# Attention of a small vision tower on one core: keys copied in six pieces by image, keys turned behind the probabilities, output product ahead of the scores

## The chip, the cores and the metric

One core of a Trainium2 chip runs the whole kernel. The metric is the device time of one execution in microseconds (us). Within a core the engines run their own instruction queues in order and meet at semaphores: PE is TensorE (matrix products and transposes), PEld its weight loads, DVE is VectorE, ACT is ScalarE, POOL is GpSimd, SP is SyncE, which issues most DMAs.

## The reference, cut to what matters

```python
h = tokens(x)                      # 32 images x 38 rows of 256: two class rows, 36 patches
h = h + attn(layernorm(h))         # 16 heads of 16
h = h + ffn(layernorm(h))          # 8 experts, two for each row, rotation, gate

def attn(x):                       # N = 32, L = 38, H = 16, D = 16
    q, k, v = x @ Wq.T, x @ Wk.T, x @ Wv.T      # each split into heads
    q, k = layernorm(q, gq, bq), layernorm(k, gk, bk)   # over the 16 of a head
    scores = where(causal, q @ k.T, -1e30)
    return softmax(scores) @ v @ Wo.T + bo
```

All of it is in fp32. The change touches `attn` alone, and there only who copies the keys and in which order the work of several tiles is issued.

## The kernel before, in words

The rows are worked in NT = 11 tiles of three images (114 rows; the last has two images). Embedding, the projections of all tiles and most of the head norms come first. Then attention runs as a software pipeline over tiles, and after it come the second norm, the experts in 26 slots, the rotation and the output.

In attention each engine runs its own `attn_step(t)` for t = 0 to 10: tiles 0 and 1 written out, 2 to 7 in a loop of two tiles a turn, 8 to 10 written out. For a tile:

- POOL multiplies the queries with their reciprocal deviations into three copies, one for each image (`norm`, L283 on POOL), spreads the values (`spread`, L431) and adds up the three images of the result (`gather_images`, L442, L443). DVE does the same to the keys (`norm_k`, L283 on DVE).
- PE transposes queries (`turn_q`, L1379) into PSUM banks 0 and 1, keys (`turn_k`, L1393) into banks 2 and 3: eight blocks of 96 rows, image i in partitions 32i to 32i+31.
- ACT copies the queries to `qd_sb` in three pieces, one for each image, 32 partitions by 304 (`keep_q`, L563). The keys go to `kc_sb`; there each image has two copies, a = 0 and a = 1, whose scales and biases blank the other head of a pair. ACT copies bank 2 (the first four blocks) in six pieces of 32x152 (`keep_k`, L572), three for a = 0 ahead of the probability copies and three for a = 1 behind them; DVE copies bank 3 in six pieces (`keep_k`, L893). `ka_kept` and `kv_kept` count the tiles that ACT and DVE have kept.
- PE makes the scores in two halves (`scores`, L1403 the mask, L1406 the products), in banks 4 and 5; DVE takes the row maximum and subtracts it (`shift`, L925, L927); ACT takes the exponential of each half (`exp_half`, L580).
- PE transposes the probabilities (`turn_probs`, L1417) into banks 0 and 1, ACT copies them in two parts (`keep_pT`, L586, L588), PE multiplies with the values (`values`, L1430), DVE divides by the sums and picks each row's image (`select`, L940, L943, L948).
- PE transposes the result (`turn_att`, L1313, on `att_sb`) into bank 2, ACT copies it (`keep_attT`, L594), PE multiplies with Wo into bank 3 (`output`, L1448), and DVE adds the residual and takes statistics (`finish`, L931, L779).

Banks 2 and 3 are thus shared: keys of tile t+2, then the turned result of tile t-1, and the output of tile t-2. The waits keep them apart: `turn_att(t)` waits for `ka_kept` of tile t+3, `output(t)` for `kv_kept` of tile t+4, `turn_k` for the copies of the turned result and for the residual add of earlier tiles.

What sets the order is the written order of the steps on each engine. Before the change it is, on PE: turn_q(t+2), turn_k(t+2), scores(t+1), turn_probs(t), output(t-2), values(t), turn_att(t-1). On ACT: keep_q(t+2), keys a = 0 of t+2, keep_pT(t), keys a = 1, exp halves of t+1, keep_attT(t-1), and in steps 8 and 9 a scaling of the generators (L615). On DVE: keep_k(t+2), shift(t+1), finish(t-2), norm_k(t+3), select(t).

Of the kernel before, what the change touches and what calls it, by code (L numbers as in the profile page):

```python
# [13 lines left out]
B, SEQ, D = 32, 38, 256  # L14
IPT = 3
# [44 lines left out]
def vit_kernel(nc, patches, w_tok, w_qkv, w_o, w_pre, w1, w2, b2, gens, gens_t,  # L60
# [6 lines left out]
    with ctx:  # L67
# [137 lines left out]
        q_kept, ka_kept, kv_kept, v_spread = sem("q_kept"), sem("ka_kept"), sem("kv_kept"), sem("v_spread")  # L205
# [76 lines left out]
        def scaled(eng, dst, src, r):  # L282
            return eng.tensor_tensor(wide(dst), thrice(src), r.unsqueeze(2).broadcast_to([T, NH * IPT, HD]), ALU.mult)  # L283

# [231 lines left out]
        def _(act):  # L516
# [50 lines left out]
            def keep_k(t, s, a):  # L567
                act.wait_ge(k_turned, t + 1)
                for i in range(IPT):
                    r, c = slice(32 * i, 32 * i + 32), slice(SEQ * i, SEQ * (i + 1))  # L570
                    kc = kc_sb[r, s * CH:s * CH + CH // 2].rearrange("p (n a m) -> p n a m", a=2, m=SEQ)
                    last = nc.scalar.activation(kc[:, :, a, :], bank[2][r, :].rearrange("p (n m) -> p n m", m=128)[:, :, c], ACT.Identity,  # L572
                                                scale=col_sb[r, C_GK + a:C_GK + a + 1], bias=col_sb[r, C_BK + a:C_BK + a + 1])
                if a == 1:
                    last.then_inc(ka_kept, 1)
# [20 lines left out]
            def attn_step(t, s):  # L596
                if ahead(t, 2):
                    keep_q(t + 2, s)
                    keep_k(t + 2, s, 0)
                keep_pT(t)  # L600
                if ahead(t, 2):
                    keep_k(t + 2, s, 1)
                if ahead(t, 1):
                    exp_half(t + 1, 1 - s, 0)
                    exp_half(t + 1, 1 - s, 1)
                if behind(t, 1):
                    keep_attT(t - 1)
# [10 lines left out]
            for t in range(EARLY, NT):  # L618
# [3 lines left out]
                if t == 9:  # L622
                    keep_k(0, 0, 0)
            keep_k(0, 0, 1)
# [5 lines left out]
            keep_k(1, 1, 0)  # L630
            keep_k(1, 1, 1)
# [124 lines left out]
        def _(dve):  # L756
# [127 lines left out]

            def keep_k(t, s):
# [3 lines left out]
                for i in range(IPT):  # L889
                    r, c = slice(32 * i, 32 * i + 32), slice(SEQ * i, SEQ * (i + 1))  # L890
                    kc = kc_sb[r, s * CH + CH // 2:(s + 1) * CH].rearrange("p (n a m) -> p n a m", a=2, m=SEQ)
                    for a in range(2):
# [875 lines left out]
```

## Time and profile before

| what | value |
|---|---|
| median of 3 runs | 359.38 us (359.34 to 362.27) |
| the profiled execution | 359.24 us, span 356.7 us, mean granted clock 0.966 |
| PE busy | 320.9 us, 90% |
| DVE busy | 219.9 us, 62% |
| ACT busy | 184.6 us, 52% |
| POOL busy | 140.8 us, 39% |

The profile cuts the span into 40 equal slices of 8.9 us; a digit is the busy share of a slice in tenths:

```profile
PE   5999999729999999987989599999999999998794
DVE  0275467997789999987888478776322212113674
ACT  0212455846688989855423785243434556550451
POOL 2001815041445665373004248757752644522000
PEclk9999999955799999999999999999999999999999
```

Attention lies in slices 8 to 17, about 70 to 160 us. The busy shares are averages over stages; starts of instructions, a tile apart, say more of one stage.

### The profile page before, as it was taken

To read this page: it belongs to the slowest core of one execution; us is meant where nothing else is said; L and a number is where in the kernel's file an instruction comes from. 1 tells how busy PE (TensorE), PEld (TensorE's weight loads), DVE (VectorE), ACT (ScalarE), POOL (GpSimd) and SP (SyncE) were. 2 spreads that over 40 slices of the span, in tenths; PEclk is the share of its full clock that TensorE was granted. 3 is DMA by queue.
4 is the path that set the end of the run, shared out by engine and by line. 5 is a ranking of instruction groups with operands and counts; after the bars stand their busy time and mean duration, and the time that the engine had idled before them with its cause. 6 is when DMAs were issued, how large, how long until landed. Compare 5 with 4: busy or idle time off the path is not lost.

```text
span 356.7 us, 6514 instructions
## 1 busy us (share of the span) xinstructions
PE 320.9 (90%) x1954; PEld 272.7 (76%) x1954; DVE 219.9 (62%) x590; ACT 184.6 (52%) x432; POOL 140.8 (39%) x147
## 2 busy tenths in 40 slices
PE   5999999729999999987989599999999999998794
PEld 4987556528888888875778498899988999986673
DVE  0275467997789999987888478776322212113674
ACT  0212455846688989855423785243434556550451
POOL 2001815041445665373004248757752644522000
PEclk9999999955799999999999999999999999999999
DMA  8571411123111110009622366535442567641443
GB/s 253 195 275 55 187 56 56 55 91 131 48 47 48 47 46 17 2 1 408 237 90 80 95 210 178 174 108 169 131 157 75 180 193 194 200 137 59 144 145 103
DMA packets 21120, 45.29 MB, mean 127 GB/s; under 512 B 2086, under 2 KB 14436, under 8 KB 20836
## 3 DMA queue, kind: packets, MB, share of 16 engines
q1 hardware_dynamic: 17444, 36.79, 31.3%
q0 software_dynamic: 2496, 6.82, 6.2%
q10 hardware_dynamic: 1152, 1.32, 1.2%
q8 instruction: 15, 0.25, 0.3%
q14 instruction: 13, 0.11, 0.1%
HBM read 37.71 MB, written 7.22 MB: 126 GB/s over the span
## 4 chain that ended last, share of the span: by engine, by line
PE 71%; issue 7%; DMA 6%; DVE 5%; SPq 3%; ACT 3%; POOL 3%; DVEq 0%; POOLq 0%; ACTq 0%
PE banks L1573 11%; PE banks L1582 10%; PE banks L1515 9%; PE banks L1289 7%; PE banks L1430 6%; PE banks L1406 5%; SPq L372 3%; PE banks L1334 3%; PE banks L1448 3%; PE banks L1379 3%; PE banks L1393 3%; DMA qk_sb<-y_rows 3%; PE banks L1486 2%; DMA qn_sb<-z_rows,gidx_sb 2%; PE banks L1417 2%
## 5 line engine op out<-in xcount | busy, mean ns | idle before, releaser
L1573 PE MATMUL banks<-qn_sb,w_sb 128*128 128x128 f32 x416 | 51.1, 276 | 1.2 <-ACT qn_sb L671 1.0
L1573 PEld LDWEIGHTS banks<-qn_sb,w_sb 128*128 128x128 f32 x416 | 48.6, 192 | 2.1 <-ACT qn_sb L671 1.2
L1582 PE MATMUL banks<-w_sb,sq_sb 128*128 x208 | 49.0, 379 | 0.0
L671 ACT ACTIVATE qn_sb<-banks,col_sb 128x128 f32<-128x128 f32 x52 | 21.0, 454 | 43.9 <-PE banks L1560 39.8
L1204 DVE TENSOR_TENSOR pT_sb<-banks,p_sb 128x256 f32<-128x256 f32 x26 | 11.0, 424 | 52.0 <-PE banks L1582 45.9
L484 POOL DMA_INDIRECT y_rows<-pT_sb,sidx_sb x26 | 25.7, 990 | 43.4 <-DVE pT_sb L1204 42.5
L1582 PEld LDWEIGHTS banks<-w_sb,sq_sb 128*128 128x128 f32 x208 | 38.1, 190 | 4.4
L682 ACT ACTIVATE sq_sb<-banks,col_sb 128x128 f32<-128x128 f32 x104 | 32.3, 364 | 16.4 <-PE banks L1573 13.7
L478 POOL DMA_INDIRECT qn_sb<-z_rows,gidx_sb x26 | 27.9, 1073 | 20.5 <-PE banks L1560 11.5
L572 ACT ACTIVATE kc_sb<-banks,col_sb 32x152 f32<-32x152 f32 x66 | 31.0, 470 | 1.1
L1289 PE MATMUL banks<-patch_sb,wtok_sb 128*128 128x252 f32 (+1 forms) x120 | 26.1, 380 | 4.3 <-DMA wtok_sb<-in_w_tok 4.3
L1289 PEld LDWEIGHTS banks<-patch_sb,wtok_sb 128*128 128x128 f32 x120 | 22.7, 207 | 6.6 <-DMA wtok_sb<-in_w_tok 4.3
L893 DVE TENSOR_SCALAR kc_sb<-banks,col_sb 32x152 f32<-32x152 f32 x66 | 25.5, 423 | 2.6 <-PE banks L1393 2.3
L563 ACT ACTIVATE qd_sb<-banks,col_sb 32x304 f32<-32x304 f32 x33 | 19.7, 597 | 10.9 <-PE banks L1379 10.6
L442 POOL TENSOR_TENSOR att_sb<-p_sb 114x256 f32<-114x256 f32 x11 | 8.1, 738 | 38.8 <-DVE p_sb L948 38.8
L1430 PEld LDWEIGHTS banks<-vd_sb,pT_sb 114*114 114x114 f32 x132 | 19.1, 188 | 5.3 <-issue 3.9
L283 POOL TENSOR_TENSOR qn_sb<-qk_sb,wtok_sb 114x768 f32<-114x768 f32 x11 | 17.1, 1562 | 14.4 <-DVE wtok_sb L868 7.4
L1430 PE MATMUL banks<-vd_sb,pT_sb 114*114 114x147 f32 x132 | 20.9, 302 | 1.8 <-ACT pT_sb L586 1.8
L1406 PE MATMUL banks<-kc_sb,qd_sb 96*114 96x76 f32 x176 | 22.2, 275 | 0.0
L1406 PEld LDWEIGHTS banks<-kc_sb,qd_sb 96*114 96x114 f32 x176 | 22.2, 197 | 0.0
L1334 PE MATMUL banks<-wqkv_sb,h_sb 128*114 128x512 f32 x44 | 20.7, 592 | 0.0
L1379 PE MATMUL banks<-con_sb,qn_sb 114*96 114x114 f32 x88 | 12.1, 288 | 6.6 <-POOL qn_sb L283 6.6
(234 smaller groups left out, 635.2 us busy)
## 6 DMA issues: line engine op xcount, KB each, us to landing
w_sb<-in_w SPq DMA_DIRECT2D x26, 512.0 KB
w_sb<-in_w SPq DMA_DIRECT2D x1, 4096.0 KB, 12.7
vrep_sb<-v_rows SPq DMA_DIRECT2D x33, 114.0 KB
qk_sb<-y_rows SPq DMA_DIRECT2D x10, 228.0 KB
patch_sb<-in_patches SPq DMA_DIRECT2D x3, 756.0 KB, 4.4
v_rows<-v_sb SPq DMA_DIRECT2D x11, 114.0 KB
z_rows<-h_sb SPq DMA_DIRECT2D x11, 114.0 KB
out_rows<-h_sb SPq DMA_DIRECT2D x10, 114.0 KB
```

Source lines behind the costliest of these rows:

```text
L478: pool.indirect_dma_start(out=xs_sb[:, s * D:(s + 1) * D], out_offset=None, in_=z_dram, in_offset=bass.IndirectOffsetOnAxis(ap=gidx_sb[:, ...
L484: pool.indirect_dma_start(out=y_dram, out_offset=bass.IndirectOffsetOnAxis(ap=sidx_sb[:, j:j + 1], axis=0), in_=ys_sb[:, s * D:(s + 1) * D ...
L572: last = nc.scalar.activation(kc[:, :, a, :], bank[2][r, :].rearrange("p (n m) -> p n m", m=128)[:, :, c], ACT.Identity, scale=col_sb[r, C ...
L682: last = nc.scalar.activation(hidT_sb[:, s * HID + c * 128:s * HID + (c + 1) * 128], bank[2 + 2 * s + c // 2][:, (c % 2) * 128:(c % 2 + 1) ...
L893: last = nc.vector.tensor_scalar(kc[:, :, a, :], bank[3][r, :].rearrange("p (n m) -> p n m", m=128)[:, :, c], col_sb[r, C_GK + a:C_GK + a ...
L1289: return nc.tensor.matmul(embed_out(g, c), wtok_sb[:, k * D + c * 128:k * D + (c + 1) * 128], patch_sb[:, at + k * w:at + (k + 1) * w], st ...
L1334: last = nc.tensor.matmul(bank[4 + s][0:T, :], hT(t, k), wqkv_sb[:, k * 3 * D:k * 3 * D + 2 * D], start=(k == 0), stop=(k == 1))
L1406: last = nc.tensor.matmul(bank[4 + hf][0:T, n * 2 * SEQ:(n + 1) * 2 * SEQ], qd_sb[0:96, q0:q0 + T], kc_sb[0:96, k0:k0 + 2 * SEQ], start=Fa ...
L1430: last = nc.tensor.matmul(bank[6 + n // 3][0:T, n % 3 * IPT * VW:(n % 3 * IPT + w) * VW], pT_sb[0:w * SEQ, n * T:(n + 1) * T], vd_sb[0:w * ...
L1515: last = nc.tensor.matmul(dst[:, m * D:(m + 1) * D], xT[:, k * D + m * 128:k * D + (m + 1) * 128], y[:, k * D:(k + 1) * D], start=(k == 0) ...
L1573: last = nc.tensor.matmul(bank[2 + 2 * s + c // 2][:, (c % 2) * 128:(c % 2 + 1) * 128], w1_sb[:, w0:w0 + 128], xsT_sb[:, (2 * s + k) * 128 ...
L1582: last = nc.tensor.matmul(bank[6 + s][:, 0:D], hidT_sb[:, s * HID + k * 128:s * HID + (k + 1) * 128], w2_sb[:, ds(e * 4 * D + k * D, D)], ...
```

## The change

The keys of a tile are copied by image instead of by bank. A piece is now 32x304, over both banks: ACT takes image 0 (a = 0 and 1) and image 2 with a = 0, DVE image 2 with a = 1 and then image 1 with a = 0 and 1. A new semaphore, `k2_kept`, holds ACT's piece of image 2 until DVE's piece of the same image is done. Both key semaphores are now asked for in scores, output and turn_att. The order of the steps becomes, on PE: turn_q(t+2), output(t-2), scores(t+1), turn_probs(t), turn_k(t+2), values(t), turn_att(t-1); on ACT: keep_q(t+2), exp half 0 of t+1, keep_pT(t), exp half 1, keep_k(t+2), keep_attT(t-1); on DVE: finish(t-2), shift(t+1), keep_k(t+2), norm_k(t+3), select(t).

```diff
--- before.py
+++ after.py
@@ -202,7 +202,7 @@
         qk_made, v_made, qk_squared_cr, v_kept_cr, ss_set_cr = (
             sem("qk_made"), sem("v_made"), sem("qk_squared_cr"), sem("v_kept_cr"), sem("ss_set_cr"))
         rs_set, qn_set, kn_set, q_turned, k_turned = sem("rs_set"), sem("qn_set"), sem("kn_set"), sem("q_turned"), sem("k_turned")
-        q_kept, ka_kept, kv_kept, v_spread = sem("q_kept"), sem("ka_kept"), sem("kv_kept"), sem("v_spread")
+        q_kept, ka_kept, kv_kept, k2_kept, v_spread = sem("q_kept"), sem("ka_kept"), sem("kv_kept"), sem("k2_kept"), sem("v_spread")
         scored, shifted_cr, max_set, probs_set = sem("scored"), sem("shifted_cr"), sem("max_set"), sem("probs_set")
         p_turned, pT_kept, pv_made, rc_set, rci_set, sel_set = (
             sem("p_turned"), sem("pT_kept"), sem("pv_made"), sem("rc_set"), sem("rci_set"), sem("sel_set"))
@@ -282,6 +282,11 @@
         def scaled(eng, dst, src, r):
             return eng.tensor_tensor(wide(dst), thrice(src), r.unsqueeze(2).broadcast_to([T, NH * IPT, HD]), ALU.mult)
 
+        def k_part(s, i, a):
+            r = slice(32 * i, 32 * i + 32)
+            dst = kc_sb[r, s * CH:(s + 1) * CH].rearrange("p (n a m) -> p n a m", a=2, m=SEQ)[:, :, a, :]
+            return banks[1][r, :].rearrange("p (n m) -> p n m", m=128)[:, :, SEQ * i:SEQ * (i + 1)], dst, r
+
         def ahead(t, n):
             return not isinstance(t, int) or t + n < NT
 
@@ -564,15 +569,17 @@
                                                 scale=col_sb[r, C_GQ:C_GQ + 1], bias=col_sb[r, C_BQ:C_BQ + 1])
                 last.then_inc(q_kept, 1)
 
-            def keep_k(t, s, a):
+            def keep_k_part(s, i, a):
+                src, dst, c = k_part(s, i, a)
+                return nc.scalar.activation(dst, src, ACT.Identity, scale=col_sb[c, C_GK + a:C_GK + a + 1],
+                                            bias=col_sb[c, C_BK + a:C_BK + a + 1])
+
+            def keep_k(t, s):
                 act.wait_ge(k_turned, t + 1)
-                for i in range(IPT):
-                    r, c = slice(32 * i, 32 * i + 32), slice(SEQ * i, SEQ * (i + 1))
-                    kc = kc_sb[r, s * CH:s * CH + CH // 2].rearrange("p (n a m) -> p n a m", a=2, m=SEQ)
-                    last = nc.scalar.activation(kc[:, :, a, :], bank[2][r, :].rearrange("p (n m) -> p n m", m=128)[:, :, c], ACT.Identity,
-                                                scale=col_sb[r, C_GK + a:C_GK + a + 1], bias=col_sb[r, C_BK + a:C_BK + a + 1])
-                if a == 1:
-                    last.then_inc(ka_kept, 1)
+                keep_k_part(s, 0, 0)
+                keep_k_part(s, 0, 1)
+                act.wait_ge(k2_kept, t + 1)
+                keep_k_part(s, 2, 0).then_inc(ka_kept, 1)
 
             def exp_half(t, s, hf):
                 act.wait_ge(shifted_cr, 2 * t + hf + 3)
@@ -596,13 +603,13 @@
             def attn_step(t, s):
                 if ahead(t, 2):
                     keep_q(t + 2, s)
-                    keep_k(t + 2, s, 0)
-                keep_pT(t)
-                if ahead(t, 2):
-                    keep_k(t + 2, s, 1)
                 if ahead(t, 1):
                     exp_half(t + 1, 1 - s, 0)
+                keep_pT(t)
+                if ahead(t, 1):
                     exp_half(t + 1, 1 - s, 1)
+                if ahead(t, 2):
+                    keep_k(t + 2, s)
                 if behind(t, 1):
                     keep_attT(t - 1)
                 if isinstance(t, int) and t in (8, 9):
@@ -620,15 +627,13 @@
                 if t == 8:
                     keep_q(0, 0)
                 if t == 9:
-                    keep_k(0, 0, 0)
-            keep_k(0, 0, 1)
+                    keep_k(0, 0)
             root(1)
             nc.scalar.activation(al_sb[:, 78:79], con_sb[:, K_ZERO:K_ZERO + 1], ACT.Exp)
             keep_q(1, 1)
             exp_half(0, 0, 0)
             exp_half(0, 0, 1)
-            keep_k(1, 1, 0)
-            keep_k(1, 1, 1)
+            keep_k(1, 1)
             attn_tiles(act, attn_step)
 
 
@@ -882,17 +887,18 @@
                 k, r = qk_sb[0:T, ds(t * 2 * D + D, D)], rs_sb[0:T, ds((2 * t + 1) * RW, RW)]
                 scaled(nc.vector, kn_sb[0:T, s * IPT * D:(s + 1) * IPT * D], k, r).then_inc(kn_set, 1)
 
+            def keep_k_part(s, i, a):
+                src, dst, c = k_part(s, i, a)
+                return nc.vector.tensor_scalar(dst, src, col_sb[c, C_GK + a:C_GK + a + 1], col_sb[c, C_BK + a:C_BK + a + 1],
+                                               ALU.mult, ALU.add)
+
             def keep_k(t, s):
                 dve.wait_ge(k_turned, t + 1)
                 if behind(t, 2):
                     dve.wait_ge(scored, 2 * t - 2)
-                for i in range(IPT):
-                    r, c = slice(32 * i, 32 * i + 32), slice(SEQ * i, SEQ * (i + 1))
-                    kc = kc_sb[r, s * CH + CH // 2:(s + 1) * CH].rearrange("p (n a m) -> p n a m", a=2, m=SEQ)
-                    for a in range(2):
-                        last = nc.vector.tensor_scalar(kc[:, :, a, :], bank[3][r, :].rearrange("p (n m) -> p n m", m=128)[:, :, c],
-                                                       col_sb[r, C_GK + a:C_GK + a + 1], col_sb[r, C_BK + a:C_BK + a + 1], ALU.mult, ALU.add)
-                last.then_inc(kv_kept, 1)
+                keep_k_part(s, 2, 1).then_inc(k2_kept, 1)
+                keep_k_part(s, 1, 0)
+                keep_k_part(s, 1, 1).then_inc(kv_kept, 1)
 
             for t in range(EARLY):
                 qkv_step(t, t % 2)
@@ -955,12 +961,12 @@
                 stats(h1_sb, t)
 
             def attn_step(t, s):
+                if behind(t, 2):
+                    finish(t - 2)
+                if ahead(t, 1):
+                    shift(t + 1, 1 - s)
                 if ahead(t, 2):
                     keep_k(t + 2, s)
-                if ahead(t, 1):
-                    shift(t + 1, 1 - s)
-                if behind(t, 2):
-                    finish(t - 2)
                 if ahead(t, 3):
                     norm_k(t + 3, 1 - s)
                 if isinstance(t, int) and t == NT - 1:
@@ -1386,8 +1392,8 @@
                     pe.wait_ge(kv_kept, t)
                 if behind(t, 4):
                     pe.wait_ge(attT_kept, t - 3)
-                if behind(t, 5):
-                    pe.wait_ge(h1_added_c1, t - 3)
+                if behind(t, 4):
+                    pe.wait_ge(h1_added_c1, t - 2)
                 for n in range(NH // 2):
                     at = s * IPT * D + n * 96
                     last = nc.tensor.transpose(banks[1][0:96, n * 128:n * 128 + T], kn_sb[0:T, at:at + 96], identT)
@@ -1397,8 +1403,9 @@
 
             def scores(t, s):
                 pe.wait_ge(q_kept, t + 1)
+                pe.wait_ge(ka_kept, t + 1)
+                pe.wait_ge(kv_kept, t + 1)
                 for hf in range(2):
-                    pe.wait_ge(ka_kept if hf == 0 else kv_kept, t + 1)
                     pe.wait_ge(shifted_cr, 2 * t + hf + 1)
                     nc.tensor.matmul(bank[4 + hf][0:T, 0:CH // 2], idb_sb[0:T, :], mask8, start=True, stop=False, skip_group_check=True)
                     for n in range(4):
@@ -1436,12 +1443,14 @@
                 pe.wait_ge(att_set, t + 1)
                 if more:
                     pe.wait_ge(ka_kept, t + 4)
+                    pe.wait_ge(kv_kept, t + 4)
                 turn_two(bank[2], att_sb[0:T, s * D:(s + 1) * D]).then_inc(att_turned, 1)
 
             def output(t, more=True):
                 pe.wait_ge(attT_kept, t + 1)
                 if more:
-                    pe.wait_ge(kv_kept, t + 5)
+                    pe.wait_ge(ka_kept, t + 4)
+                    pe.wait_ge(kv_kept, t + 4)
                 if behind(t, 1):
                     pe.wait_ge(h1_added_c1, t + 1)
                 for k in range(2):
@@ -1452,12 +1461,13 @@
             def attn_step(t, s):
                 if ahead(t, 2):
                     turn_q(t + 2, s)
-                    turn_k(t + 2, s)
+                if behind(t, 2):
+                    output(t - 2, ahead(t, 1))
                 if ahead(t, 1):
                     scores(t + 1, 1 - s)
                 turn_probs(t, s)
-                if behind(t, 2):
-                    output(t - 2, ahead(t, 2))
+                if ahead(t, 2):
+                    turn_k(t + 2, s)
                 values(t, s)
                 if behind(t, 1):
                     turn_att(t - 1, 1 - s, ahead(t, 2))
```

## Rows read from the trace of the kernel before

**Rows 1.** Stretches: start:end, length, busy us of each engine, clock, DMA share, GB/s.

```profile
127.95:135.37 7.42, 7.14 (x61) 6.45 (x61) 7.08 (x19) 6.58 (x14) 4.33 (x4) 1.00 0.14 46
```

**Rows 2.** Timeline of DVE, one tile: start us, us, line, operation.

```profile
128.96 1.02 DVE L948 TENSOR_TENSOR p_sb<-banks,rci_sb 114x432 f32<-114x432 f32 x2
...
129.90 2.35 DVE L893 TENSOR_SCALAR kc_sb<-banks,col_sb 32x152 f32<-32x152 f32 x6
...
132.28 0.47 DVE L925 TENSOR_REDUCE mx_sb<-banks 114x8 f32<-114x304 f32 x1
...
132.78 0.47 DVE L927 TENSOR_TENSOR p_sb<-banks,mx_sb 114x304 f32<-114x304 f32 x1
...
134.06 0.41 DVE L931 TENSOR_TENSOR h_sb<-banks,hb_sb 114x256 f32 x1
...
136.37 1.02 DVE L948 TENSOR_TENSOR p_sb<-banks,rci_sb 114x432 f32<-114x432 f32 x2
```

**Rows 3.** Timeline of PE, same tile; PE busy times overlap, ends are modelled.

```profile
127.54 0.41 PE L1313 MATMUL banks<-con_sb,att_sb 114*128 114x114 f32 x2
...
127.85 0.98 PE L1379 MATMUL banks<-con_sb,qn_sb 114*96 114x114 f32 x8
...
129.53 0.29 PE L1403 MATMUL banks<-maskb_sb,idb_sb 114*114 114x304 bf16 x1
...
131.32 0.75 PE L1417 MATMUL banks<-con_sb,p_sb 114*114 114x114 f32 x6
...
132.35 1.09 PE L1448 MATMUL banks<-wo_sb,attT_sb 128*114 128x256 f32 x4 [0.28 <-issue]
...
133.27 1.75 PE L1430 MATMUL banks<-vd_sb,pT_sb 114*114 114x147 f32 x12
...
134.95 0.41 PE L1313 MATMUL banks<-con_sb,att_sb 114*128 114x114 f32 x2
...
135.20 0.94 PE L1379 MATMUL banks<-con_sb,qn_sb 114*96 114x114 f32 x8
```

**Rows 4.** Timeline of ACT, same tile.

```profile
128.96 1.82 ACT L563 ACTIVATE qd_sb<-banks,col_sb 32x304 f32<-32x304 f32 x3 [0.61 <-PE banks L1379]
...
132.25 0.55 ACT L586 ACTIVATE pT_sb<-banks 114x456 f32<-114x456 f32 x1
...
133.08 1.44 ACT L572 ACTIVATE kc_sb<-banks,col_sb 32x152 f32<-32x152 f32 x3
...
134.54 0.80 ACT L580 ACTIVATE p_sb<-p_sb 114x304 f32<-114x304 f32 x2
...
135.48 0.36 ACT L594 ACTIVATE attT_sb<-banks 128x228 f32<-128x228 f32 x1
```

**Rows 5.** Chain of waits, tiles 2 and 8 to 10: start us, us, what.

```profile
103.79 1.58 PE banks L1430 x12
...
148.26 1.59 PE banks L1430 x12
...
153.44 1.58 PE banks L1430 x12
...
155.66 1.33 ACT wqkv_sb L615
...
157.13 0.55 ACT pT_sb L586
...
157.81 1.82 PE banks L1430 x12
```

**Rows 6.** Timeline of PE and DVE, first scores.

```profile
67.91 0.31 PE L1403 MATMUL banks<-maskb_sb,idb_sb 114*114 114x304 bf16 x1 [2.01 <-ACT kc_sb L572]
...
69.09 0.47 DVE L925 TENSOR_REDUCE mx_sb<-banks 114x8 f32<-114x304 f32 x1 [0.18 <-PE banks L1406]
```

**Rows 7.** Timeline of PE, values of tiles 0 and 1.

```profile
86.17 3.31 PE L1430 MATMUL banks<-vd_sb,pT_sb 114*114 114x147 f32 x12 [0.35 <-ACT pT_sb L586]
...
96.19 1.81 PE L1430 MATMUL banks<-vd_sb,pT_sb 114*114 114x147 f32 x12 [0.54 <-ACT pT_sb L586]
```

## The prediction, made before the changed kernel was run

> **What bounds the kernel now.** I read the slices of the page first, to find the stage that the change touches; then the table of stretches for five tiles of it; then the timelines of VectorE (DVE), TensorE (PE) and ScalarE (ACT) over one of these tiles, start against start; then the chain of waits, to see how the stage begins and ends. The change acts only on attention. In its steady part a tile takes 7.41 to 7.42 us, and in that time DVE is busy 7.08, PE 7.14 by modelled ends, ACT 6.58 and POOL 4.33 [rows 1]. Busy shares that close together don't name the bound; the starts do.
>
> On DVE the starts of a period are: select 128.96, keys 129.90, max 132.28, residual add 134.06, next select 136.37 [rows 2]. That is 0.94 + 2.38 (six key pieces) + 1.78 (shift of two halves) + 2.31 (add, statistics, norm of the next keys, reciprocals) = 7.41, the whole period, with no wait for another engine in it. So DVE sets the pace. PE shows what that does to the others: the probabilities are turned at 131.32, which takes 0.59 for six transposes, and the output product starts only at 132.35, 0.44 later [rows 3]; it stands behind its wait for the last key piece, which DVE ends at 129.90 + 2.35 = 132.25 [rows 2]. The page puts this down to "issue", because the wait sits on an instruction of its own. Without that hole PE would need about 7.41 - 0.44 = 6.97 a tile. The stage lies on the chain of waits from end to end: between the values products of tiles 2 and 8 there are six periods, 103.79 to 148.26, and tiles 9 and 10 follow at 153.44 and 157.81 [rows 5].
>
> **The change, part by part.** *Key copies on DVE.* Six pieces of 32x152 go (2.38) and three of 32x304 come. Such a piece on DVE isn't in the trace. Below I bound it by the 0.47 of the 114x304 shift [rows 2], above by two old pieces, 2 x 2.38 / 6 = 0.79. I take 0.55, nearer the row with the same element count and the same source memory. DVE saves 2.38 - 1.65 = 0.73 a tile (0 to 0.97 at the ends). Its period by itself becomes 6.7.
>
> *Key copies on ACT.* Six pieces at 0.48 (three start and end in 1.44) become three like the query copies, same 32x304 shape, scale and bias, 1.82 for three [rows 4]. ACT saves about 1.1. The third ACT piece also waits for DVE's piece of the same image, k2_kept. Even if both engines start their keys at once, DVE's piece takes 0.55 and ACT's two pieces before the wait take 1.2, so they hide it; I cost it at nothing. If DVE came a full 0.79 piece later than ACT, 0.4 of it would show.
>
> *Order on PE.* The same products are issued; only places change. Added waits (both key semaphores in the scores, in the output and in turn_att) cost nothing where the semaphore is long up. Three places matter. (a) turn_k moves behind turn_probs, ahead of the values: it fills the time in which ACT copies the turned probabilities. (b) output(t-2) comes between turn_q and the scores. (c) turn_att(t-1) writes the bank that the keys of tile t+2 are read from, so it waits for those keys. Before, they were turned a whole step earlier in the queue; now they are turned just ahead of the values, and ACT copies them last: query copy, exp half, two probability copies, exp half, and only then the keys. What queues behind turn_att on PE is everything of the next step, turn_q, output and scores.
>
> *The ring that this closes.* Take PE's turn_att as start. turn_att to turn_q 0.25 (134.95 to 135.20), turn_q 0.84 (half of 127.85 to 129.53), output 0.92 (132.35 to 133.27) [rows 3]. From the first product of the first scores half to the max that reads it 1.18 (67.91 to 69.09) [rows 6]. On DVE max to end of shift 0.97 (132.28 to 132.78, then 0.47) [rows 2]. On ACT exp half 0.36 to 0.40, the two probability copies 0.83 (132.25 to 133.08), exp half 0.36 to 0.40, three key pieces 1.82 [rows 4]. Two handoffs, DVE to ACT and ACT to PE, 0.13 at most each (157.13 + 0.55 to 157.81) [rows 5]; I take 0.1. Sum: 0.25 + 0.84 + 0.92 + 1.18 + 0.97 + 0.36 + 0.83 + 0.36 + 1.82 + 0.2 = 7.73, against 7.41 now. None of DVE's saving is in it: the ring holds none of the DVE key pieces. ACT's shorter copies are in it, but earlier they were beside the ring. So six periods cost 6 x 0.32 = **+1.9**. In the trace this is a hole on PE ahead of turn_att: the values start when the first probability copy is down, 0.68 after that copy starts, and the keys are kept 0.83 + 0.36 + 1.82 + 0.1 = 3.1 after it, so turn_att starts 2.4 to 2.5 after the values instead of 1.68 (133.27 to 134.95) [rows 3].
>
> *Tile 9.* No turn_q is left to fill. From values(8): turn_att(7) 2.45; to ACT's copy 0.53 and the copy 0.36 + 0.13 (134.95, 135.48) [rows 3, 4]; output(7) 0.92; scores half to max 1.18; to end of shift 0.97; handoff 0.1; exp half 0.40, because it stands ahead of the probability copy in ACT's queue; first copy and handoff 0.68; values(9). Sum 7.7 against 5.18 now. I take **+2.4**, as the handoffs at 0.13 are upper values. Before, the scores of tile 10 came first and the output filled the wait for the copy.
>
> *Tile 10.* values(9) to turn_att(8) 1.68, copy of it 1.02, output(8) 0.92, turn_probs 0.6, first copy 0.68: 4.9 against 4.37 (153.44 to 157.81) now. The copy now also waits behind the scaling of the generators (155.66 and 157.13) [rows 5], which ends as early as before, so it adds nothing. **+0.5**.
>
> *The first tiles.* PE ran tile 0 and most of tile 1 at half the granted clock, 1.2 GHz (the two slices of the page with a 5), and waited 0.35 and 0.54 for probability copies [rows 7]; turn_k now fills these. Between nothing and 0.89, I take **-0.5**. The stage starts when POOL has the queries of tile 2, which nothing in the change touches. POOL and the DMA queues carry the same work with slack: POOL is idle for over 3 of 7.42 us [rows 1].
>
> Sum: +1.9 + 2.4 + 0.5 - 0.5 = +4.3. What follows the stage waits for tile 10's values through select, so it moves one for one. The profiled execution took 359.24 us (span 356.7); that makes 363.5, and as the median of the runs, 359.38, stands 0.14 above it, I don't move the sum for that. I take off 0.2 for the handoffs, which are upper values in the ring too: **363.3 us**.
>
> **The rivals.** *1. The saturated engine is relieved and the kernel follows.* For it: DVE has no slack now and loses 0.73. Then the ring of turn_att must be short, which it is if ACT reaches its keys early: the first exp half would have to find its shift ready well before. The period would be PE's 6.97: 6 x -0.44 = -2.6, tile 9 without the hole ahead of turn_att 7.7 - 0.77 - 5.18 = +1.7, tile 10 +0.5, first tiles -0.5: -0.9, 358.3 us. It decides from the point where the ring falls under 7.41, that is, 0.32 shorter than summed. Against it: each term of the ring has a row, and they overlap nowhere. The Trainium skill, Perfetto Trace Analysis, section Optimizing Scalar/DVE Operations, says that each operation carries a fixed access cost and that "Grouping and performing larger operations can improve throughput if the engine is saturated". The trace agrees that DVE is saturated here; this rival is what the rule would give.
>
> *2. The ring is shorter than summed, the tail is as summed.* If the copies start a little ahead of my handoffs the period stays at 7.4 to 7.6: 0 to +1.1, and with tail and first tiles +1.5 to +3: 361 to 362.3 us. For it: ends on PE are modelled, and the 1.18 comes from another stage.
>
> *3. Waits cost PE's queue.* When turn_att stands still, the waits of turn_q, output and scores behind it can't be worked off beside running products. Turn_att to turn_q already varies from 0.25 to 0.31 (127.54 to 127.85) [rows 3]; with up to 0.28 more, the size of the wait that the page calls issue, the period would be 8.0: +1.6 more, 365.0 us. The clock could add to it: PE's rise to 2.4 GHz after tile 1's start could come later, each microsecond late costing half of one.
>
> *4. The key pieces on DVE cost 0.79 each*: DVE's load is then 7.41, still under the ring. No change of the sum.
>
> **How the numbers follow.** Forecast (+2.9 to +5) 0.60, rival 2 0.20, rival 3 0.10, rival 1 0.10. The range 360.3 to 366.0 takes in the forecast, rival 2, rival 3's middle value and leaves out rival 1 and long clock delays, 0.15 to 0.2 in all. Within 1% of 359.38 means 355.8 to 363.0, which is about what a measurement of this kernel can tell from no change. Faster by more: rival 1 would have to beat its own price, 0.05. Slower by more: forecast cases above +3.6, about two thirds of them, and rival 3: 0.50. Within: 0.45.
>
> **What would show it.** PE idle ahead of turn_att, some 0.8 in each tile, released by ACT's keys; no hole ahead of the output; tile periods of 7.6 to 7.9; values(8) to values(9) above 7; DVE key pieces three for each tile at 0.5 to 0.6 and DVE idle around 0.7 a tile. The forecast is wrong if turn_att starts 1.7 after the values, or if ACT waits for PE ahead of its keys.

## The result, and the profile after

| | before | changed |
|---|---|---|
| median, same chip | 361.0 us (20 runs, 356.83 to 365.16) | 359.95 us (20 runs, 358.53 to 364.43) |
| the profiled execution | 359.24 us | 359.96 us |
| its span, mean granted clock | 356.7 us, 0.966 | 357.3 us, 0.975 |
| PE, DVE, ACT busy | 320.9, 219.9, 184.6 us | 318.8, 215.2, 170.4 us |

The ratio of the times, changed to before, is **1.0053, with a 95% interval of 1.0027 to 1.0078**. Executions that a slower state of the chip disturbed are left out of it, which is why it can be above 1 while the median of all runs is lower. On the 359.38 us of the prediction that makes 361.3 us (360.4 to 362.2). The forecast was 363.3 with a range of 360.3 to 366.0: slower, and inside the range, but by half of what the sum said. The prediction had put 0.50 on slower by more than 1% and 0.45 on within 1%; the result is within.

The slices of the page after, to be set against those of before. Each digit is the busy share of 8.9 us in tenths; the last row is PE's granted clock:

```profile
PE   5999999629999989977989599999999999998794
DVE  0275477996988989957888478776322222113484
ACT  0211455825767766655423785243434556550351
...
PEclk9999999956999999999999999999999999999899
```

Two things differ. DVE and ACT are less busy in attention, as the copies promised. And the clock row has a 5 and a 6 where before it had 5, 5 and 7. I compared the starts of the values products in both timelines, which cut the stage into the terms of the sum:

| stretch | before | changed | difference | forecast |
|---|---|---|---|---|
| start to values(0) | 86.17 | 85.68 | -0.49 | -0.5, with the next row |
| values(0) to (2) | 17.46 | 14.39 | **-3.07** | |
| values(2) to (8), six periods | 44.47 (7.41 each) | 46.06 (7.68 each) | +1.59 | +1.9 |
| values(8) to (9) | 5.18 | 7.22 | +2.04 | +2.4 |
| values(9) to (10) | 4.53 | 4.85 | +0.32 | +0.5 |
| to the first product of the next stage | 2.00 | 1.99 | 0 | 0 |
| sum | 159.81 | 160.19 | +0.38 | +4.3 |

The steady part and the tail came out close to the forecast. The first tiles gave back nearly all of it. The experts after the stage take 118.65 us before and 118.41 after, and a stretch of low clock at 335.7 to 339.1 us, which before did not have, costs some tenths, so that the spans end 0.6 apart.

One steady tile of the changed kernel, from the timeline of all engines; it answers to [rows 2 to 4]. Columns: start us, us, engine, line, operation, and in brackets the idle time before it and who ended it:

```profile
127.66 0.29 PE L1410 MATMUL banks<-maskb_sb,idb_sb 114*114 114x304 bf16 x1
...
128.92 0.46 DVE L931 TENSOR_REDUCE mx_sb<-banks 114x8 f32<-114x304 f32 x1
...
129.91 0.46 ACT L587 ACTIVATE p_sb<-p_sb 114x304 f32<-114x304 f32 x1 [1.00 <-DVE p_sb L933]
...
131.00 1.84 PE L1437 MATMUL banks<-vd_sb,pT_sb 114*114 114x147 f32 x12
131.08 0.46 ACT L587 ACTIVATE p_sb<-p_sb 114x304 f32<-114x304 f32 x1
131.14 1.72 DVE L892 TENSOR_SCALAR kc_sb<-banks,col_sb 32x304 f32<-32x304 f32 x3 [0.37 <-PE banks L1399]
131.43 1.68 ACT L574 ACTIVATE kc_sb<-banks,col_sb 32x304 f32<-32x304 f32 x3
...
133.21 0.39 PE L1319 MATMUL banks<-con_sb,att_sb 114*128 114x114 f32 x2 [0.37 <-ACT kc_sb L574]
133.52 0.98 PE L1385 MATMUL banks<-con_sb,qn_sb 114*96 114x114 f32 x8
...
134.34 1.03 PE L1457 MATMUL banks<-wo_sb,attT_sb 128*114 128x256 f32 x4
...
135.21 0.29 PE L1410 MATMUL banks<-maskb_sb,idb_sb 114*114 114x304 bf16 x1
```

Read it as the ring of the prediction. PE turns the result at 133.21, 0.10 after ACT's keys end (131.43 + 1.68 = 133.11); it starts 2.21 after the values, where before it was 1.68. DVE's keys had ended at 132.86, 0.25 earlier. The output follows turn_q with no hole (134.34), where before PE stood 0.44 ahead of it [rows 3]. And DVE now waits 0.37 ahead of its keys, where before it waited for nobody [rows 2].

The waits of 100 to 150 us say how often: wait, us in total, times, longest.

```profile
DVE kc_sb L892 <- PE banks L1399: 2.3, 7, 0.4
PE banks L1319 <- ACT kc_sb L574: 2.3, 7, 0.4
```

The same wait stands in all seven tiles of this stretch.

### The profile page after: what moved, and what is told of

It reads as the page before. It is cut to its first block, busy times and chain, and to the rows that moved or that the text cites. A ratio compares the mean times of both kernels' runs of the same rounds, so it can differ in the third digit from the quotient of the medians.

```text
span 357.3 us, 6456 instructions
## 1 busy us (share of the span) xinstructions
PE 318.8 (89%) x1954; PEld 270.3 (76%) x1954; DVE 215.2 (60%) x557; ACT 170.4 (48%) x399; POOL 140.6 (39%) x147
## 3 DMA queue, kind: packets, MB, share of 16 engines
q0 software_dynamic: 2496, 6.82, 6.3%
HBM read 37.71 MB, written 7.22 MB: 126 GB/s over the span
## 4 chain that ended last, share of the span: by engine, by line
PE 66%; DVE 13%; issue 9%; ACT 6%; DMA 3%; POOL 3%; DVEq 1%; SPq 0%; ACTq 0%; POOLq 0%
PE banks L1525 11%; PE banks L1583 11%; PE banks L1592 10%; PE banks L1295 7%; PE banks L1340 3%; PE banks L1671 3%; PE banks L1496 2%; DMA qn_sb<-z_rows,gidx_sb 2%; PE banks L1413 2%; PE banks L1437 2%; PE banks L1385 2%; ACT kc_sb L574 2%; POOL qn_sb L283 2%; PE banks L1457 2%; PE banks L1570 1%
## 5 line engine op out<-in xcount | busy, mean ns | idle before, releaser
L1437 PEld LDWEIGHTS banks<-vd_sb,pT_sb 114*114 114x114 f32 x132 | 17.6, 181 | 5.8 <-issue 3.7
L892 DVE TENSOR_SCALAR kc_sb<-banks,col_sb 32x304 f32<-32x304 f32 x33 | 18.5, 585 | 4.8 <-PE banks L1399 4.4
L574 ACT ACTIVATE kc_sb<-banks,col_sb 32x304 f32<-32x304 f32 x33 | 18.4, 588 | 1.4 <-PE banks L1399 0.8
```

The source lines that it names most:

```text
L574: return nc.scalar.activation(dst, src, ACT.Identity, scale=col_sb[c, C_GK + a:C_GK + a + 1], bias=col_sb[c, C_BK + a:C_BK + a + 1])
L1437: last = nc.tensor.matmul(bank[6 + n // 3][0:T, n % 3 * IPT * VW:(n % 3 * IPT + w) * VW], pT_sb[0:w * SEQ, n * T:(n + 1) * T], vd_sb[0:w * ...
```

## The experiments

My theory: the ring that goes through ACT's keys into turn_att sets the period and the longer tail, and the missing cost is the clock of the first tiles. The rivals: DVE or PE sets the pace by its load, or the new copies are what costs.

**ACT's keys ahead of the second exp half.** This takes one exp half out of the ring and leaves every load as it is.

```diff
 ACT attn_step:  keep_q, exp half 0, keep_pT,
-                exp half 1, keep_k, keep_attT
+                keep_k, exp half 1, keep_attT
```

> The changed kernel with one move on ACT: a tile's three key pieces ahead of the second exp half instead of behind it. Ring theory (turn_att waits for ACT's keys, and everything of the next step on PE stands behind it): one exp half, 0.36 us, leaves the ring, so the tile period falls from 7.68 to about 7.3 us, the hole ahead of turn_att from about 0.5 to 0.2, and over the steps to tile 8 some 2 us are saved; tiles 9 and 10 keep 7.2 and 4.85. Rival theory (DVE or PE's own load sets the pace and the wait ahead of turn_att is only idle time that would stand elsewhere): period stays at 7.6 to 7.7.

Measured: the period fell from 7.68 to 7.45 us; tiles 9 and 10 stayed at 7.22 and 4.85. The ratio to before was 0.9983 (0.9938 to 1.0028), 360.19 us. The timeline of this kernel, one tile:

```profile
130.21 1.68 ACT L574 ACTIVATE kc_sb<-banks,col_sb 32x304 f32<-32x304 f32 x3
130.26 1.71 DVE L892 TENSOR_SCALAR kc_sb<-banks,col_sb 32x304 f32<-32x304 f32 x3 [0.37 <-PE banks L1399]
...
132.12 0.39 PE L1319 MATMUL banks<-con_sb,att_sb 114*128 114x114 f32 x2 [0.15 <-DVE kc_sb L892]
```

The releaser of turn_att changes from ACT to DVE. The ring through ACT is shown; only 0.23 of the 0.35 came back, because DVE's keys were 0.25 behind it as the next thing that turn_att waits for.

**The new copies in the old order.** All three step orders of before, with the six pieces by image.

```diff
-PE: turn_q, output, scores, turn_probs, turn_k, values, turn_att
+PE: turn_q, turn_k, scores, turn_probs, output, values, turn_att
 (ACT and DVE likewise; ACT copies all keys ahead of keep_pT)
```

> Only the new key copies (three pieces on ACT, three on DVE, by image), with the orders of the kernel before on PE, ACT and DVE; ACT copies its keys right behind the queries. Ring theory worked for this order: the output waits for both key copies, ACT does query pieces 1.8, key pieces 1.7, probability copy one after the other; the period is 7.4 to 7.5, so no gain though DVE is relieved by 0.65 us a tile. Rival (DVE was the only bound): the period falls to PE's 6.97 and the kernel is 3 to 4 us faster than before.

Measured: a period of 7.56 us, a little above the 7.4 to 7.5 expected, tail 5.18 and 4.54 as before, ratio 0.9938 (0.9845 to 1.003), 361.58 us. DVE was relieved by 0.65 a tile, and the period didn't follow; the interval of the times is too wide to decide it alone. The timeline shows what took DVE's place:

```profile
132.62 1.70 ACT L574 ACTIVATE kc_sb<-banks,col_sb 32x304 f32<-32x304 f32 x3
...
134.41 1.09 PE L1455 MATMUL banks<-wo_sb,attT_sb 128*114 128x256 f32 x4 [0.61 <-issue]
```

The output overwrites the bank from which ACT now also reads keys: it starts 0.09 after ACT's last piece (132.62 + 1.70 = 134.32). Rival 1 of the prediction, in which relief of the saturated engine is handed on, is refuted in this order as in the other.

**The new order with the old copies.** Twelve pieces of 32x152, six on each engine, in the new order.

```diff
-ACT: 3 x 32x304, DVE: 3 x 32x304
+ACT: 6 x 32x152 (bank 2), DVE: 6 x 32x152 (bank 3)
```

> Only the new orders, with the six old pieces on ACT and six on DVE by bank. Ring theory: ACT's keys in the ring take 2.9 instead of 1.7 us, so the period is 7.68 + 1.2 = 8.9, and the kernel is some 8 us slower than the changed one. Rival (the new order is harmless, the copies cost): the period stays near 7.5.

Measured in one run: 387.8 us, a period of 10.22 us, tail 11.39 and 7.88. PE's turn_att of one tile, and two stretches (start:end, length, busy us of PE, PEld, DVE, ACT, POOL, granted clock, DMA share, GB/s):

```profile
126.74 0.61 PE L1326 MATMUL banks<-con_sb,att_sb 114*128 114x114 f32 x2 [1.57 <-ACT kc_sb L583]
```

```profile
116.19:119.61 3.42, 3.13 (x13) 2.59 (x14) 1.75 (x6) 1.07 (x4) 1.41 (x2) 0.50 0.14 47
119.61:126.43 6.82, 5.54 (x47) 4.91 (x45) 5.46 (x13) 5.27 (x12) 2.93 (x3) 1.00 0.10 29
```

ACT's six pieces take 2.88 instead of 1.68, and turn_att waits for them 1.57: that part of the ring is as expected. The rest of the miss, 10.22 against 8.9, I put down to the clock, which no run here took out of this kernel: of each period 3.42 us ran at half of it, which by the length of the stretch is worth up to 1.7 us. The tail is inflated too, since the clock stayed at 0.50 from 167.39 us to the end of the stage. None of the theories had that. It shows that the new order is affordable only with the new copies.

**DVE's key pieces halved.** Six instructions of 32x152 in place of three; ACT as in the changed kernel.

```diff
-tensor_scalar(dst, src, ...)
+for n in (0, 4): tensor_scalar(dst[:, n:n + 4], src[:, n:n + 4], ...)
```

> The changed kernel with each of DVE's three key pieces issued as two halves: DVE works 0.65 us more a tile, as much as the change had taken from it. Ring theory: DVE's pieces are beside ACT's longer part, the period stays within 0.1 of 7.68. Rival (DVE is still the bound): period 8.3.

Measured in one run: 363.77 us, a period of 8.01, tail 7.69 and 4.85. Both numbers were missed: the ring's (within 0.1 of 7.68) and the load's (8.3).

```profile
134.46 2.28 DVE L893 TENSOR_SCALAR kc_sb<-banks,col_sb 32x152 f32<-32x152 f32 x6 [0.37 <-PE banks L1401]
134.75 1.68 ACT L574 ACTIVATE kc_sb<-banks,col_sb 32x304 f32<-32x304 f32 x3
...
136.89 0.39 PE L1321 MATMUL banks<-con_sb,att_sb 114*128 114x114 f32 x2 [0.73 <-DVE kc_sb L893]
```

I had left out that the ring has two branches which meet in turn_att. DVE's pieces grew by 2.28 - 1.72 = 0.56; 0.25 of it was slack, and 0.56 - 0.25 = 0.31 goes through. The period grew by 0.33. The three DVE pieces of the changed kernel are thus nearly on the ring.

**The last two steps in the old manner.** Steps 9 and 10 turn the probabilities first and issue the output behind, with ACT's and DVE's steps to match.

```diff
+late = t >= NT - 2
-if behind(t, 2): output(t - 2)
+if behind(t, 2) and not late: output(t - 2)
 ... turn_probs(t)
+if late: output(t - 2)
```

> The changed kernel, with steps 9 and 10 alone in the old manner: output behind the turned probabilities on PE, probability copy ahead of the exp half on ACT, residual add behind the shift on DVE. Tail theory: values(8) to values(9) falls from 7.22 to about 5.9 (the hole ahead of turn_att(7) stays, 0.3 to 0.5), values(9) to values(10) to about 4.6; the tile period up to tile 8 stays 7.68. Rival (the tail is long because the keys of tile 10 come late, not because of the order of output and copy): 7.2 and 4.85 stay.

Measured in one run: 358.5 us, tiles 9 and 10 at 5.63 and 4.53, the period unchanged (7.68); the first product of the next stage at 158.60 instead of 160.19. The tail is as theory has it, tile 9 a little shorter than the 5.9 expected, and 1.6 us of the change's cost was avoidable in two steps (1.9 in the two tiles; this execution entered the stage 0.3 later).

**Both kernels with PE kept busy ahead of tile 0.** 18 products into a bank that nobody reads, 4 ahead of the first scores and 14 behind. They hold the granted clock at 1.00 through the first tiles in both kernels, and so take it out of the comparison.

```diff
+keep_busy(4)     # 128x512 products, PSUM bank 7
 scores(0, 0)
+keep_busy(14)
```

> The kernel before, with 18 products of 128x512 into a bank that nothing reads, where PE stood idle before the first attention steps (4 ahead of the first scores, 14 behind the keys of tile 1). They change no output. Clock theory: the granted clock stays at 2.4 GHz through the first tiles or rises earlier; values(0) to values(2), 17.5 us with the low clock, falls toward 15, and the kernel is 3 to 8 us faster. Rival (the low clock there does not come from PE's idle time): no change, or slower by the added products.

> The same 18 products in the changed kernel. If the changed kernel was only 0.5% slower instead of 1.1% because its clock rose some 7 us earlier, then with the clock out of play in both the changed kernel is 3.0 to 4.5 us slower than the kernel before with the same products. Rival (the first tiles gained from the order itself, not from the clock): the two differ by under 1 us.

The products cost time of their own: the 14 take 12.20 us, and the queries of tile 2 come at 84.89 instead of 77.94. So the expectation for before failed in its total: values(0) to (2) fell from 17.46 to 14.21, but the kernel became 0.6% slower and not 3 to 8 us faster. What counts is the one kernel against the other:

| stretch | before + 18 | changed + 18 | difference |
|---|---|---|---|
| start to values(0) | 89.87 | 89.18 | -0.69 |
| values(0) to (2) | 14.21 | 14.37 | +0.16 |
| values(2) to (8) | 44.50 | 46.11 | +1.61 |
| values(8) to (9), (9) to (10) | 5.17, 4.54 | 7.21, 4.85 | +2.04, +0.31 |
| to the next stage | 160.29 | 163.71 | **+3.42** |

Ratios to before: 1.0058 (1.0022 to 1.0093) and 1.0153 (1.0058 to 1.0248), 361.36 and 364.7 us. At equal clock in the first tiles the change costs 1.0153 / 1.0058 = 1.0094, 3.4 us, as expected. The second interval is wide, so the times alone would not carry this; the traces do, and two runs at a mean clock of 1.000 read 358.31 and 361.98, 3.67 apart. The gain of values(0) to (2), -3.07 without the products, is +0.16 with them: it is the clock.

**The result turned early.** Could the ring be opened and the gain kept? turn_att(t-1) moves ahead of turn_probs(t), so that it waits for the keys of a whole tile earlier; exp halves move behind ACT's keys, norm_k to the end of DVE's step, and the last two steps are in the old manner.

```diff
-PE: turn_q, output, scores, turn_probs, turn_k, values, turn_att
+PE: turn_q, output, scores, turn_att, turn_probs, turn_k, values
```

> The new copies and the new order, with what closed the ring taken out: turn_att(t-1) goes ahead of turn_probs(t), so it waits for the keys of tile t+1, kept long before; turn_k(t+2) waits for its copy; ACT copies the turned result, the probabilities and the keys before both exp halves; DVE's norm of the next keys goes behind select; steps 9 and 10 in the old manner as in the run before. Ring theory: no hole ahead of turn_att, the period falls to PE's own 7.0 to 7.2 us, the tail is 5.3 and 4.7; the kernel is 4 to 6 us faster than the changed one and 2 to 4 faster than before. Rival (PE's added waits or another engine hold the period at 7.4 or more whatever the order): no gain over the kernel before.

Measured: a period of 7.82, not 7.0 to 7.2; tail 5.44 and 4.53; ratio 1.0012 (0.9968 to 1.0056), 360.97 us, so no gain over before. The timeline names the new wait:

```profile
128.47 0.95 DVE L283 TENSOR_TENSOR kn_sb<-qk_sb,wtok_sb 114x768 f32 x1
128.63 1.38 POOL L447 TENSOR_TENSOR att_sb<-p_sb 114x256 f32<-114x256 f32 x1 [2.73 <-DVE p_sb L956]
...
130.86 0.41 PE L1324 MATMUL banks<-con_sb,att_sb 114*128 114x114 f32 x2 [0.61 <-POOL att_sb L448]
```

turn_att now waits for POOL's sum of the images, whose first addition takes 1.38 instead of 0.73 where DVE's norm runs beside it.

**The norm in DVE's hole.** The same kernel with norm_k between the shift and the keys, beside POOL's spread of the values.

```diff
 DVE: finish, shift,
+     norm_k(t + 3),
      keep_k, select
-     norm_k(t + 3)
```

> The kernel of the run with the result turned early, with one move on DVE: the norm of the next keys between shift and key pieces instead of behind select. There DVE stood idle for 0.9 us in each tile, and behind select it ran beside POOL's gather of the images, whose first addition took 1.38 us instead of 0.73 while PE waited for it. Ring theory (select, gather, turn_att, turn_probs, turn_k, values is the ring of that kernel): the gather falls to 1.45 us in all, the period from 7.82 to about 7.2, and the kernel is 3 to 4 us faster than that one. Rival (the gather's length has nothing to do with DVE, or another wait follows at once): period 7.6 or more.

```profile
126.40 0.73 POOL L447 TENSOR_TENSOR att_sb<-p_sb 114x256 f32<-114x256 f32 x1 [2.10 <-DVE p_sb L956]
...
127.99 0.41 PE L1324 MATMUL banks<-con_sb,att_sb 114*128 114x114 f32 x2
...
129.02 1.18 DVE L283 TENSOR_TENSOR kn_sb<-qk_sb,wtok_sb 114x768 f32 x1
...
129.35 2.19 POOL L436 TENSOR_TENSOR vd_sb<-vrep_sb,con_sb 114x768 f32<-114x768 f32 x1
```

Measured: a period of 7.22, as expected. The addition is back at 0.73 and turn_att no longer waits on PE. The next stage starts at 156.29 in the profiled execution, 3.5 us before that of before. The ratio is 0.9983 (0.9915 to 1.0052), 357.7 us of four runs, so timing alone doesn't show the gain. Of the 3.5 us the profiled span keeps 1.8 (354.9 against 356.7): behind attention it has two stretches of 3.4 us with a clock of 0.50, at 196.62 and 333.15, and before has none there.

**The same, with PE busy early.** One product ahead of the first scores and nine behind, into the unread bank; and for comparison the kernel before with two and seven.

```diff
+keep_busy(1)
 scores(0, 0)
+keep_busy(9)
```

> The same kernel with ten products of 128x512 into a bank that nothing reads, one ahead of the first scores and nine behind the keys of tile 1, in PE's idle time; they change no output. They take 0.87 us each and end before the queries of tile 2 are there. If a high clock in the first tiles is to be had without delaying them, tiles 0 and 1 take about 7 us each at 2.4 GHz: 7 to 9 us faster than the kernel before (350 to 353 us). Rival (the clock falls anyway in that stretch): within 2 us of the run without these products.

> The kernel before with nine such products (two ahead of the first scores, seven behind the keys of tile 1). If the clock is held: 352 to 354 us, that is 6 to 7 us faster than before, and 2 to 4 slower than the run beside it, which has the new copies and the shorter period. Rival (clock falls anyway): within 1 us of the kernel before.

The first: **354.28 us (351.75 to 357.59), ratio 0.9866 (0.979 to 0.9941)**, the one kernel here whose interval lies wholly below 1; somewhat above the 350 to 353 expected. Its first queries in the timeline, and two stretches:

```profile
78.41 0.98 PE L1390 MATMUL banks<-con_sb,qn_sb 114*96 114x114 f32 x8 [0.41 <-POOL qn_sb L283]
```

```profile
78.41:89.40 10.99, 9.16 (x81) 8.48 (x82) 10.59 (x21) 6.87 (x13) 4.69 (x5) 1.00 0.37 124
89.40:92.80 3.40, 3.40 (x19) 3.36 (x18) 2.49 (x3) 1.83 (x5) 3.19 (x2) 0.50 0.14 46
```

Here the nine products run from 70.10 to 78.0, in time for the queries (0.5 later than before), and the clock is low for 3.4 us only; two runs at a mean clock of 1.000 read 352.23 and 351.75.

Not all of this gain is the products'. In the profiled execution values(0) starts 3.4 us earlier than without them (82.78 against 86.17), but the next stage only 0.25 earlier (156.04 against 156.29). Part of what was won in the first tiles was lost in one tile behind them, where DVE's norm met POOL's spread and took 2.27 us instead of 1.27, and the output waited for the keys behind it:

```profile
98.71 1.48 POOL L436 TENSOR_TENSOR vd_sb<-vrep_sb,con_sb 114x768 f32<-114x768 f32 x1
...
98.73 2.27 DVE L283 TENSOR_TENSOR kn_sb<-qk_sb,wtok_sb 114x768 f32 x1
...
103.01 1.09 PE L1462 MATMUL banks<-wo_sb,attT_sb 128*114 128x256 f32 x4 [0.96 <-DVE kc_sb L894]
```

The other 1.5 of the 1.7 us between the two profiled spans (353.2 and 354.9) lie behind attention, where this execution has one stretch of low clock (331.71 to 335.12) and the one without products two.

Before with nine products missed its 352 to 354. Its four runs read 356.0, 362.04, 363.86 and 366.59 us, at mean clocks of 0.995, 0.976, 0.966 and 0.957, and no ratio could be formed. The profile is that of the run of 362.04:

```profile
88.58 0.98 PE L1393 MATMUL banks<-con_sb,kn_sb 114*96 114x114 f32 x8 [3.09 <-DVE kn_sb L283]
```

PE waits 3.09 us for DVE's keys of the next tile, and the clock is at 0.50 from 89.8 to 106.9. The run of 356.0 has no profile. So how much of the 1.3% the products would bring to before alone is not settled.

## Why the prediction was half right

**The ring (+1.9 forecast, +1.59 measured): right in mechanism.** PE stands 0.3 to 0.4 ahead of turn_att in every tile, released by ACT's keys; I had written some 0.8, which is the whole delay of turn_att, while part of it is still covered by the values products. Summed again from the tile above: turn_att to turn_q 0.31, turn_q 0.82, output 0.87, scores to max 1.26, max to end of shift 0.96, handoff 0.03, exp 0.49, probability copies 0.68, exp 0.35, keys 1.68, handoff 0.10: 7.55. The forecast's terms that were too large are the keys (1.82, read from the query copies) and the probability copies (0.83). But turn_att to turn_att is 7.54 only within a turn of the two-tile loop. At the head of a turn it is 7.9, from the timeline of PE:

```profile
125.30 0.39 PE L1319 MATMUL banks<-con_sb,att_sb 114*128 114x114 f32 x2 [0.31 <-ACT kc_sb L574]
125.98 0.98 PE L1385 MATMUL banks<-con_sb,qn_sb 114*96 114x114 f32 x8 [0.30 <-issue]
```

Turn_q follows after 0.68 there and after 0.31 to 0.43 elsewhere, twice in the six periods (the other at 109.82 and 110.53). That is rival 3's price, a queue that can't be worked off while its head waits, in two tiles of six instead of all: 4 x 7.54 + 2 x 7.93 = 46.0. So of the +1.59, some 0.8 is the ring and 0.8 is this. That it is the loop's branch is read from where it stands, and was not tried by itself.

**Tile 9 (+2.4, measured +2.04) and tile 10 (+0.5, +0.32): right**, and shown by the old manner of the last steps. The chain is the one of the sum. The timeline of the tail, which answers to [rows 5]:

```profile
148.25 0.39 PE L1319 MATMUL banks<-con_sb,att_sb 114*128 114x114 f32 x2 [0.30 <-ACT kc_sb L574]
...
149.09 1.12 PE L1457 MATMUL banks<-wo_sb,attT_sb 128*114 128x256 f32 x4 [0.45 <-ACT attT_sb L601]
...
152.31 0.46 ACT L587 ACTIVATE p_sb<-p_sb 114x304 f32<-114x304 f32 x1 [1.68 <-DVE p_sb L933]
...
153.35 1.81 PE L1437 MATMUL banks<-vd_sb,pT_sb 114*114 114x147 f32 x12 [0.76 <-ACT pT_sb L593]
```

The sum was 0.3 too large already at turn_att (2.12 after the values at 146.13, not 2.45), and most of the rest is turn_att to output, 0.84 (148.25 to 149.09) where the sum had 0.53 + 0.49. For tile 10 the working took 4.37 as the time of before from the chain of waits, where the timeline has 4.53; the 4.9 itself was right (4.85).

**DVE (0.55 a piece taken, 0.57 to 0.58 measured) and PE's hole ahead of the output: right.** Three pieces take 1.72 and six had taken 2.35 [rows 2]. Nothing of it reached the period, in the old order either. The Trainium skill, Perfetto Trace Analysis, section Optimizing Scalar/DVE Operations, says that larger operations can improve throughput where the engine is saturated. On DVE alone the trace agrees, 0.63 a tile less; the kernel gained nothing from it, since a ring through other engines was next.

**The first tiles (-0.5 forecast, -3.56 measured): this is the step that failed.** The half that I did price, turn_k filling the hole ahead of values(0), is right: values(0) starts 0.49 earlier, and with the clock out of play the first two rows give -0.69 + 0.16 = -0.53. That the second agrees so closely is partly luck, since at full clock before waits 0.87 ahead of both values, not 0.35 and 0.54. What I gave a sentence only, and in one direction only, was the clock: rival 3 says that the rise to 2.4 GHz "could come later". It came earlier. Stretches of the changed kernel:

```profile
69.86:72.86 3.00, 0.00 (x0) 0.00 (x0) 2.92 (x5) 2.92 (x7) 0.00 (x0) 1.00 0.22 71
72.86:86.51 13.65, 8.50 (x44) 8.47 (x45) 9.97 (x21) 4.36 (x10) 4.87 (x3) 0.50 0.39 127
86.51:93.75 7.24, 7.00 (x60) 6.30 (x58) 6.65 (x16) 5.45 (x12) 3.35 (x4) 1.00 0.15 48
```

and the same of before:

```profile
69.86:72.86 3.00, 1.45 (x9) 1.07 (x6) 2.95 (x7) 2.91 (x7) 0.00 (x0) 0.50 0.17 53
72.86:86.51 13.65, 8.22 (x41) 7.82 (x42) 12.96 (x30) 6.46 (x14) 5.03 (x3) 0.50 0.39 130
86.51:93.75 7.24, 7.24 (x35) 6.84 (x35) 3.13 (x9) 4.48 (x10) 2.50 (x3) 0.50 0.14 48
```

The clock fell to 0.50 (1.2 GHz) at 69.86 before and at 72.86 after, and rose to 1.00 (2.4 GHz) at 93.75 before and at 86.51 after. In the third stretch PE issued 60 products instead of 35 in the same time. My own price, half of a microsecond for each, makes 7.24 / 2 = 3.6, against 3.07 measured.

What stays open is why the clock comes up earlier. How the two parts of the change go with it can be read, from one profiled execution of each kernel:

- The fall. With the old copies the clock fell at 69.86 us (before) and 68.41 (new order), with the new copies at 72.38 to 74.47 in all seven kernels without added products.
- The rise. In the old order it came at 93.75 (before) and 94.95 (new copies), in all seven kernels with a form of the new order at 86.03 to 88.89; the one with the old copies is the 88.89.
- The low stretch between them lasted 23.9 us in before, 20.5 with either part alone, and 13.65, to 0.1, in all six with both.

The earlier rise thus goes with the order and the later fall with the copies. Values(0) to (1) says the same: 10.02 us before, 10.01 with the copies alone, 7.30 with the order alone, 6.66 with both. Through what work of PE they do it no experiment separated. What differs ahead of the stretch is that the first scores start at 66.15 instead of 67.91, and that PE then stands idle before tile 2's queries for 9.07 us instead of 6.63.

The measured 361.3 lies in what rival 2 gave (361 to 362.3), but not for its reason: the period isn't 7.4 to 7.6. Nor does rival 2 add up: with tail and first tiles as in the sum (+2.4 + 0.5 - 0.5) its 0 to +1.1 makes +2.4 to +3.5, 361.6 to 362.7, and not +1.5 to +3. The range held because it was wide enough for two errors of opposite sign.

## What to carry to other kernels

A ring through several engines doesn't care which of them is the busiest: before relieving the saturated one, sum the next ring, and in every place where two branches meet, write down the slack of the second (here 0.25 us, which capped one repair and broke one expectation). A step moved in the first tiles moves the clock's rise as well, in either direction, and each microsecond of it is worth half of one; price it as a term with both signs. Where a kernel has a steady part and a tail, let the last steps have an order of their own: two steps in the old manner were worth 1.6 us.

## What the hardware showed that I had not expected

- With the old copies in the new order, the granted clock went to 0.50 for 3.42 us and back to 1.00 for 6.82 us, again and again, in the rhythm of the 10.2 us tiles, with a wait of PE of about 1.5 for ACT's keys in each. The waits of 0.37 in the changed kernel, and of 0.73 with DVE's pieces halved, came with nothing of the kind.
- POOL and DVE slow each other where both run a large elementwise operation, and in these rows the one that starts second pays more. DVE's norm began first (128.47, 0.95 us) and POOL's addition took 1.38 instead of 0.73; it began first again (129.02, 1.18) and POOL's product took 2.19 instead of 1.47. Where POOL's product began first by 0.02 us, it kept its 1.48 and DVE's norm took 2.27.
- ACT's key copies are shorter than its query copies of the same shape: three in 1.68 against 1.82 us. The trace doesn't say why.
- With ten products that change nothing, nine of them in a hole in which PE only waited, the clock stayed at 1.00 until 89.40 us, past the values of tile 0 at 82.78. Of the 3.4 us that values(0) came earlier in the profiled execution, 0.25 were left at the end of the stage.
